# ScalarE's output copies first in their slots, and another head: x tiles behind wv's first half, flips copied by ScalarE, statistics two tiles ahead

## The reference

```python
x = x + LN(Attn(LN(x)))     # 16 heads of 64; weights Wq, Wk, Wv, Wo
x = x + LN(Rec(LN(x)))      # below

q, k, v = (h @ W.T).reshape(N, S, 16, 64).transpose(0, 2, 1, 3)
att = softmax(einsum('nqhd,nkhd->nhqk', q, k) / 8)
out = einsum('nhqk,nkhd->nqhd', att, v)...  @ Wo.T + bo

def step(c, xt):            # scan over the 8 leading rows of x
    ft, it = sigmoid(xt @ wf.T + c @ uf.T + bf), sigmoid(xt @ wi.T + c @ ui.T + bi)
    gt = tanh(xt @ wc.T + c @ uc.T + bc)
    return ft * c + it * gt
h = tanh(x @ wo.T + c_final @ uo.T + bo)
```

## Time and profile before

| | |
|---|---|
| time, median of 3 runs | 1361.56 us (1359.27 to 1363.56) |
| the profiled execution's own time | 1356.45 us |
| span of its slowest core (core 6) | 1354.9 us |
| spans of the 8 cores | 1345.2 to 1354.9 us |
| mean granted TensorE clock, core 6 | 0.990 |
| busy share PE / DVE / ACT / POOL | 96% / 62% / 42% / 30% |
| TensorE's share of the chain that ended last | 82% |

### The profile page before, as it was taken

How to read it: one execution, slowest core, us unless ns; L and a number is a source line. 1 busy time by engine, 2 the same in 40 slices (tenths; PEclk the granted TensorE clock), 3 DMA queues, 4 the chain that set the end, 5 groups by cost and what they waited for, 6 DMA issues and landing times.

```text
span 1354.9 us, 25960 instructions; the slowest of 8 cores (1345.2 to 1354.9 us)
## 1 busy us (share of the span) xinstructions
PE 1296.4 (96%) x8256; PEld 733.4 (54%) x8256; DVE 834.1 (62%) x1460; ACT 571.9 (42%) x1572; POOL 400.9 (30%) x879
## 2 busy tenths in 40 slices
PE   4989999999899999899999999999999999999995
PEld 2577777776677777454444444444444444444442
DVE  5357778988799976574554545545455453226887
ACT  1246666665566665563222222222222222212665
POOL 3014444555455543331110101101011010001876
PEclk9999999999999999999999999999999999999998
DMA  9985676899789867728331222312222112009878
GB/s 198 197 143 115 147 152 143 190 188 184 187 196 197 203 195 266 265 71 277 128 125 47 94 91 80 125 48 94 92 80 94 48 63 78 0 15 346 272 253 248
DMA packets 126085, 200.96 MB, mean 148 GB/s; under 512 B 72672, under 2 KB 78816, under 8 KB 122848
## 3 DMA queue, kind: packets, MB, share of 16 engines
q1 hardware_dynamic: 109536, 172.56, 40.5%
q0 software_dynamic: 16416, 26.74, 14.6%
HBM read 157.34 MB, written 83.89 MB: 178 GB/s over the span
## 4 chain that ended last, share of the span: by engine, by line
PE 82%; DMA 5%; DVE 3%; SPq 3%; issue 2%; ACT 2%; POOL 2%; DVEq 0%; POOLq 0%; ACTq 0%
PE ps_big L445 11%; PE ps_s L445 11%; PE ps_s L433 11%; PE ps_big L433 11%; PE ps_big L320 11%; PE ps_big L346 7%; PE ps_big L308 6%; PE ps_big L329 3%; PE ps_s L504 3%; PE ps_big L504 2%; PE ps_o L504 2%; DMA exr<-xr 2%; PE ps_o L382 2%; SPq L1145 1%; PE ps_s L365 1%
## 5 line engine op out<-in xcount | busy, mean ns | idle before, releaser
L991 POOL TENSOR_SCALAR pn<-p,rl 128x128 bf16<-128x128 f32 x512 | 180.5, 368 | 298.2 <-DVE rl L601 297.6
L876 ACT ACTIVATE p<-ps_s,nm 128x128 f32<-128x128 f32 x512 | 181.0, 366 | 115.1 <-DVE nm L605 106.8
L346 PE MATMUL ps_big<-wo,zT 128*128 128x512 bf16 x512 | 122.9, 384 | 13.5 <-ACT zT L887 10.2
L691 DVE SCALAR_TENSOR_TENSOR ti<-ti,tg 128x512 f32<-128x512 f32 x64 | 44.2, 690 | 141.8 <-ACT tg L927 141.8
L308 PE MATMUL ps_big<-wv,xT 128*128 128x512 bf16 x512 | 123.1, 388 | 0.7 <-DVE zb L587 0.5
L320 PE MATMUL ps_big<-xT,wq 128*128 128x256 bf16 x1024 | 122.1, 274 | 0.0
L320 PE MATMUL ps_big<-xT,wk 128*128 128x256 bf16 x1024 | 121.2, 273 | 0.0
L605 DVE TENSOR_REDUCE nm<-ps_s 128x4 f32<-128x512 f32 x128 | 88.4, 691 | 29.0 <-PE ps_s L365 26.0
L876 ACT ACTIVATION_READ_ACCUMULATOR p<-ps_s,nm 128x1 f32 x512 | 104.2, 203 | 0.0
L320 PEld LDWEIGHTS ps_big<-xT,wq 128*128 128x128 bf16 x1024 | 98.2, 98 | 11.0
L320 PEld LDWEIGHTS ps_big<-xT,wk 128*128 128x128 bf16 x1024 | 97.7, 98 | 10.8
(11 more groups left out here) (162 smaller groups left out, 2479.1 us busy)
## 6 DMA issues: line engine op xcount, KB each, us to landing
z_scr<-zb SPq DMA_DIRECT2D x32, 512.0 KB, 6.2
h<-x_scr SPq DMA_DIRECT2D x29, 512.0 KB, 6.8
out<-h SPq DMA_DIRECT2D x28, 512.0 KB, 4.1
xin<-x SPq DMA_DIRECT2D x26, 512.0 KB, 6.6
zb<-z_scr SPq DMA_DIRECT2D x24, 512.0 KB, 4.2
xrb<-xr SPq DMA_DIRECT2D x24, 512.0 KB, 3.5
x_scr<-xrb SPq DMA_DIRECT2D x24, 512.0 KB, 2.9
vst<-v_scr SPq DMA_DIRECT2D x64, 128.0 KB, 6.6
```

The lines of the kernel that those rows point to most:

```text
L346: mm = t.matmul(bank[:], zT[u % 2][:, ft * 128:(ft + 1) * 128], wo[:, ft * D + half * 512:ft * D + half * 512 + 512], start=ft == 0, stop= ...
L876: ex = a.activation(p32[G % 2][:, c], psS[G % 2][:, c], AF.Exp, bias=nm[G % 2][:, pk:pk + 1], accum_out=ls[G % 2][:, pk:pk + 1])
L991: op = g.tensor_scalar(pn[G % 2][:, c], p32[G % 2][:, c], rl[G % 2][:, pk:pk + 1], 1.0, AL.mult, AL.mult)
```

## The change

- The head's loads: GpSimd's queue now carries wv's first half, then x tiles 2 to 7, then the other weights, each issued between two `rstd1`; SyncE issues only x tiles 0 and 1 and then at once the masks, the biases and `bo_bc`.
- The head's order: flips 0 and 1, then V groups 0 and 1, then each flip directly ahead of the group that reads it. The copies of flips 0 to 7 move from VectorE to ScalarE. VectorE takes statistics two tiles ahead of the normalization.
- The slots: `oevict` comes first in the odd slots instead of last.
- `xl` tiles 4 and 5 get another place (over `exr`), so ScalarE no longer waits for flips before the second F group; the cell on VectorE waits in its place (i == 4), and SyncE's load of xl waits for other semaphores.

```diff
@@ -181,7 +181,8 @@
     xl = ([at(f"xl{i}", [128, D], BF16, oXZ + 2048 * i) for i in range(4)]
-          + [xln[0], xln[1], vtok[0], vtok[1]])
+          + [at(f"xl{i}", [128, D], BF16, oXR + o) for i, o in ((4, 6144), (5, 4096))]
+          + [vtok[0], vtok[1]])
     mo = [oM]
@@ -412,11 +413,11 @@
 
-        for u in range(4):
-            flip1(u)
+        flip1(0)
+        flip1(1)
         for i, key in enumerate(head_groups()):
-            if 3 <= i < 7:
-                flip1(i + 1)
+            if 2 <= i < 8:
+                flip1(i)
             group(key)
@@ -695,16 +696,20 @@
                 v.wait_ge(d_exl, 16 * 8)
+            elif i == 4:
+                v.wait_ge(p_t2, 6)
             v.wait_ge(s_S, i + 1)
...
             v.memset(vst[i][:], 0.0).then_inc(s_ms, 1)
-        for u in range(0, 8, 2):
-            for step in (stats1, apply1, flip1_out):
-                step(u)
-                step(u + 1)
+        stats1(0)
+        stats1(1)
+        for u in range(8):
+            apply1(u)
+            if u < 6:
+                stats1(u + 2)
         v.memset(vst[2][:], 0.0).then_inc(s_ms, 1)
@@ -845,9 +850,7 @@
                     a.wait_ge(p_t2, 4)
-                elif i == 1:
-                    a.wait_ge(p_t2, 6)
-                else:
+                elif i >= 2:
                     a.wait_ge(s_S, i - 1)
@@ -895,11 +898,23 @@
         a.activation(junk[:], mhalf[:, 0:1], AF.Exp)
-        for key in head_groups():
+        def flip1_out(u):
+            n, tt = u // 4, u % 4
+            a.wait_ge(s_t1, u + 1)
+            dst = xT[n % 2][:].rearrange("p (f t) -> p f t", f=8)[:, :, tt * 128:(tt + 1) * 128]
+            a.copy(dst, psT[:].rearrange("p (f t) -> p f t", f=8)).then_inc(s_t1e, 1)
+
+        flip1_out(0)
+        flip1_out(1)
+        for i, key in enumerate(head_groups()):
+            if 2 <= i < 8:
+                flip1_out(i)
             evict(key)
...
             gs = slot_groups(G)
+            if 5 <= G < NG and G % 2 == 1:
+                oevict((G - 5) // 2)
             if len(gs) > 0:
@@ -908,9 +923,7 @@
                 post_norm((G - 32) // 8)
-            if 5 <= G < 112 and G % 2 == 1:
-                oevict((G - 5) // 2)
-            elif G >= 112 and G % 2 == 0:
+            if G >= NG and G % 2 == 0:
                 oevict((G - 4) // 2)
@@ -963,14 +976,16 @@
     def gpsimd(g):
-        for kind, dst, src in (("V", wv, wv_d), ("K", wk, wk_d), ("Q", wq, wq_d)):
-            for c in range(2):
-                g.dma_start(out=dst[:].rearrange("p (f m) -> p f m", f=8)[:, :, c * 512:c * 512 + 512],
-                            in_=src.rearrange("(f p) m -> p f m", p=128)[:, :, c * 512:c * 512 + 512]
-                            ).then_inc(d_w[f"{kind}{c}"], 16)
-        g.dma_start(out=wo[:].rearrange("p (f m) -> p f m", f=8),
-                    in_=wo_d.rearrange("(f p) m -> p f m", p=128)).then_inc(d_w["Z"], 16)
+        def wload(kind, c):
+            dst, src = {"V": (wv, wv_d), "K": (wk, wk_d), "Q": (wq, wq_d)}[kind]
+            g.dma_start(out=dst[:].rearrange("p (f m) -> p f m", f=8)[:, :, c * 512:c * 512 + 512],
+                        in_=src.rearrange("(f p) m -> p f m", p=128)[:, :, c * 512:c * 512 + 512]
+                        ).then_inc(d_w[f"{kind}{c}"], 16)
+
+        wload("V", 0)
         g.memset(mhalf[:], -0.5).then_inc(s_mh, 1)
+        for u in range(2, 8):
+            g.dma_start(out=xhead[u][:], in_=x_d[u]).then_inc(d_xh[u], 16)
         g.wait_ge(s_mh, 1)
@@ -1015,8 +1030,14 @@
 
-        for u in range(8):
-            rstd1(u)
+        rstd1(0)
+        rstd1(1)
+        for u, (kind, c) in enumerate((("V", 1), ("K", 0), ("K", 1), ("Q", 0), ("Q", 1))):
+            wload(kind, c)
+            rstd1(u + 2)
+        rstd1(7)
+        g.dma_start(out=wo[:].rearrange("p (f m) -> p f m", f=8),
+                    in_=wo_d.rearrange("(f p) m -> p f m", p=128)).then_inc(d_w["Z"], 16)
         for G in range(NG + 3):
@@ -1085,12 +1106,6 @@
         def xload_head(u):
-            if u == 2:
-                s.wait_ge(d_xh[0], 16)
-            elif u == 4:
-                s.wait_ge(d_xh[2], 16)
-            elif u == 6:
-                s.wait_ge(d_w["V0"], 16)
             s.dma_start(out=xhead[u][:], in_=x_d[u]).then_inc(d_xh[u], 16)
@@ -1175,7 +1190,7 @@
         s.dma_start(out=ident[:], in_=id_d).then_inc(d_id, 16)
-        for u in range(8):
+        for u in range(2):
             xload_head(u)
@@ -1228,7 +1243,8 @@
                     u_stage(0)
-                    s.wait_ge(s_t1, 32)
+                    s.wait_ge(p_ap, 8)
+                    s.wait_ge(d_ex1, 16 * 8)
                     s.wait_ge(d_vs[0], 16 * 12)
```

## The result

| | before | after |
|---|---|---|
| time, median of 8 runs each | 1360.8 us (1355.47 to 1363.56) | 1368.59 us |
| the profiled execution's own time | 1356.45 us | 1368.05 us |
| spans of the 8 cores | 1345.2 to 1354.9 us | 1349.4 to 1366.2 us (core 2 slowest) |

The ratio after to before is 1.0065, 95% interval 1.0048 to 1.0082. One of the eight runs of after fell in a slower state of the chip (1568.87 us, the other seven 1365.78 to 1371.73 with the median 1368.05), and such runs are left out of every ratio and interval, and of the experiments' medians. The changed kernel is slower by 7.8 us of the medians of all runs, beyond the 0.3% that a measurement can tell, and stands at the upper edge of the predicted range: 1368.59 is just past 1368.5.

A forecast was written before the change was run, and what follows sets the result against it. TensorE, busy 96% of the span, was taken to bound the kernel by its own order and waits. Head +4.0, zT waits -7.1, wc's load +1.7 made -1.4 us: 1360.2 us, 8 in 10 between 1352.5 and 1368.5.

The forecast's parts named there:

- Term 1, the landing: Head: wv's first half lands at 22.4 us, with bounds of 14.9 and 24.8 us.
- the lower bound: Head: wv's first half lands at 14.9 us if nothing of the small loads' cost falls on it.
- Term 1, "the tile's input is early enough": Head: x tile 2 lands 1.9 us behind the weight; statistics of tiles 2 and 3 finish before the first two groups.
- the forecast of no measurable change: Whole kernel: -1.4 us lies inside the 0.3% (4.1 us) a measurement can tell; no change was given 43%.
- Term 1, the starting point: Head: before's first K group starts at 60.0 us; after the change at 64.0 us, 4.0 us later.
- Term 1, the period: Head: flips of tiles 2 to 7 run in series, 3.6 us apart; six tiles make 21.6 us.
- Rival (b): Head: the serial chain falls to half clock, 5.8 us a tile; 1366.8 us, 1368 with a landing at 24; 20%.
- Term 2: Slots: all ten TensorE waits for the output copy zT go, -7.1 us, bounds 0 to -8 us.
- Rival (c): Slots: the zT copy in front delays exponentials and VectorE's copies, so the zT gain is 0; 1367 us; 6%.
- Term 3: Around wc's load: TensorE waits 5.7 us instead of 1.75, half clock behind it; +1.7 us, between 0 and 3.4.
- The load starts by the same event: wc's load: still issued when the last Q group has ended, so time won earlier becomes a longer wait, 5.7 us.
- The sum: Whole kernel: 4.0 - 7.1 + 1.7 = -1.4 us, giving a median of 1360.2 us.

The follow-up runs named there:

- e4: The changed kernel, but SyncE issues masks, biases and bo_bc only when x tile 7 has landed; ratio to the kernel before 1.0013 (0.9996 to 1.0029).
- e9: The changed kernel with tile 1's normalization ahead of tile 2's statistics on VectorE, the two-tile lead resumed behind it; ratio to before 1.0004 (0.999 to 1.0019).
- e8: The kernel before with the slot edits alone and the casts of four of eight recurrent weights left out; ratio to before 0.9932, median 1353.46 us.
- e2: The kernel before with the slot edits alone (zT copies first, xl tiles 4 and 5 moved), before's head; ratio to before 0.9994 (0.9979 to 1.001).

## Why the prediction was wrong

**Term 1, the landing: right.** Predicted 22.4 us, measured 22.3 on core 2 and 22.6 as the mean of the cores. e4 took the small loads away and found the lower bound, 14.9 predicted and 15.5 measured (14.3 to 16.8 on the cores).

**Term 1, "the tile's input is early enough": this step failed.** It asked whether x tile 2's landing is early enough for tile 2's own flip, and it is. It did not ask who else stands behind that landing. The normalization of tile 1 does on VectorE, flip 1 behind it on TensorE, and the first V group behind flip 1. The predicted sentence that x tile 2 lands 1.9 us behind the weight already held the answer: on core 2 VectorE goes on 2.8 us behind the weight's landing (25.06 - 22.3), the statistics of tile 2 take 1.5 us, tile 1's normalization 1.0 until flip 1 starts, flip 1 itself 0.8, and V starts at 28.4 instead of 22.7. As the mean of the cores it is 27.8, and this one step is 5.1 of the 8.4 us by which the predicted time was missed. e9 removes it and gets 64.3 us for the first K group, where 64.0 was predicted; against before it is even (after is at 1.0065, the intervals do not touch), which agrees with the forecast of no measurable change. Of the 5.7 us by which W comes earlier in e9 than in after, 4.1 are the head's; the rest arises in the slots, where nothing was edited.

**Term 1, the starting point.** The prediction reckoned from core 6, whose first K group starts at 60.0 us before; the mean of the cores is 58.7. Against that, 64.0 is 5.3 us later and not 4.0. With the failed step's 5.1, and 0.7 less from V to K (40.6 for 41.3), this makes the head's 9.7.

**Term 1, the period: right.** 3.62 us, with a copy of 1.01 us (1.057 taken), at full clock. Rival (b) is refuted: idling 1.29 us in each 3.6 us did not lower the granted clock (1.00 up to 52 us). The case in the Trainium skill that the prediction named for it (TensorE: Matmul & The Clock Gate, "HAM oscillation") has waits of 3 to 5 us between bursts; it spoke less for (b) than the prediction let it. That the measured time is close to (b)'s 1366.8 to 1368 us is coincidence: the mechanism did not occur.

**Term 2: the waits went, the time only in part.** Predicted -7.1 us for the stretch up to 545 us; measured from K to the first F group (541.1 us before, 545.9 after) -4.9 us, of which -3.8 up to the xl flip. Two different things took the rest. Up to 479 us, about half of the zT waits came back as waits for VectorE behind late loads; with half the casts gone (e8 against e2: 0 for 3.4 us) none comes back. Past 479 us, 3.7 of the 7.8 us of zT waits (mean of the cores) stood where the recurrent weights' loads decide when TensorE goes on. From 479 to 614 us 7.7 us of waits became only 6.8, and from xl to W the time grew by 0.4 us: what was won up to the F groups was lost at them. The prediction gave this very reason for wc in term 3, but drew the line at 545 us instead of 479. e8 left out both the traffic of the casts and GpSimd's work of issuing them, and these were not separated; the long issue on SyncE is one instance, and how much of it is queueing there and how much the transfer itself was not separated either. Rival (c), exponentials delayed by the copy in front, did not show: no wait of TensorE for exponentials is in the lists of after from 127 to 545 us.

**Term 3: right in size.** From xl to W 0.4 us was lost, and from the first F group to W 1.5 us (73.6 to 75.1), where +1.7 was predicted. The wait of 5.7 us came as 5.0, split between wi and wc on all eight cores (on core 1 0.5 and 4.4), where one wait had been predicted. "The load starts by the same event" held only nearly: wc's issue starts 3.8 us behind the last Q group instead of 0.7 (means), because the issue of the vst loads ahead of it takes longer, but it lands 17.3 us behind that group instead of 16.6.

**The sum.** Predicted 4.0 - 7.1 + 1.7 = -1.4 us. By the traces 9.7 - 4.9 + 1.5 = +6.3, by the medians of all runs +7.8. The first is the mean of the eight cores in one execution, the second the slowest core of eight runs; the 1.5 us between them were not traced to a cause.

## What to carry to other kernels

When a statement is moved ahead in an engine's program to give it a lead, look at what it waits for and what then stands behind it: an engine works in order, and one wait for a late landing holds every ready instruction that follows, on other engines too. A lead is best begun behind the last item whose input is already there (e9), not at the first place where it can be written.

A wait that is taken away is gained only up to the next thing that is due. Before adding up ten waits, sort them by what limits the stretch in which each stands: here half lay where weight loads set the pace, and of those nothing was left at W.

## What the runs showed of the hardware

- Three mask loads to eight partitions (together 393 KB), four bias vectors and a row spread to 128 partitions delay megabytes on another queue: on core 2 the mean rate from 12 to 20 us is 181 GB/s with them and 292 GB/s without, and wv's first half lands about 7 us later. By the time of wv's second half (38.7 and 38.3 us) the difference is gone.
- SyncE was held 10.89 us by issuing a single store of 512 KB in a stretch with casting DMAs. It happens past the casts too: 5.22 us for two vst loads ahead of wc's load.
- The head's TensorE, idle 1.29 us of each 3.62 us, kept the granted clock at 1.00. The length of one wait alone does not tell what follows: on core 2 of after a wait of 3.1 us had no drop behind it (1.00 to 568 us), the one of 3.3 us that followed had 0.50 from 568.2 to 574.8 us, and before, 2.22 us had 3.4 us of 0.50 behind them.
- Casting DMAs that nothing waits for cost time: leaving out half of them took 0.34% (0.12 to 0.55%) off the kernel before. Whether by their traffic or by GpSimd's work of issuing them is not shown.
